# A slot-routing layer on eight cores: weight groups loaded in iterations 8 to 14, and the middle stage rearranged

## Time and profile before

| what | value |
|---|---|
| the profiled execution's own time | 314.32 us |
| its span, core 0 (the slowest) | 312.8 us |
| spans of the eight cores | 303.3 to 312.8 us |
| busy: PE, DVE, ACT, POOL | 72%, 64%, 57%, 53% |
| DMA queue q0 (issued by POOL) | 22.22 MB, 47.4% of 16 engines' span |
| DMA queue q1 (issued by SP) | 42.28 MB, 40.7% of 16 engines' span |
| loads of tiles 0 to 7 from DRAM (848) | 4 of 1024 KB |
| stores of the output (877) | 32 of 512 KB, 9.2 us to landing |

### The profile page before, as it was taken

The page is one execution under the profiler, slowest core; times in us unless marked ns, Lnnn a source line. Parts: engine busy times, 40 slices in busy tenths (PEclk is TensorE's granted clock), DMA queues, the critical chain, the costliest instruction groups (busy, mean ns, idle before and its releaser), DMA issues.

```text
span 312.8 us, 5721 instructions; the slowest of 8 cores (303.3 to 312.8 us)
## 1 busy us (share of the span) xinstructions
PE 223.8 (72%) x1784; PEld 131.7 (42%) x1806; DVE 201.7 (64%) x358; ACT 178.5 (57%) x332; POOL 164.6 (53%) x236
## 2 busy tenths in 40 slices
PE   0114769877998973696996999999478964888700
PEld 0001347653774751475774768864143420111000
DVE  1476787998895982479996566434522316999930
ACT  0117556793795883369797799541211028999800
POOL 3774897757775960888886758212000004656510
PEclk9999589998997998599997999999959996555555
DMA  7999999999999999999997000839999594999996
GB/s 184 269 233 184 233 214 238 229 245 259 253 301 206 216 234 268 189 244 168 160 174 117 1 3 8 130 51 147 179 161 176 168 337 190 353 345 353 351 353 246
DMA packets 23792, 65.43 MB, mean 209 GB/s; under 512 B 1958, under 2 KB 2470, under 8 KB 23762
## 3 DMA queue, kind: packets, MB, share of 16 engines
q0 software_dynamic: 11376, 22.22, 47.4%
q1 hardware_dynamic: 11584, 42.28, 40.7%
q10 hardware_dynamic: 802, 0.57, 0.6%
HBM read 66.30 MB, written 20.97 MB: 279 GB/s over the span
## 4 chain that ended last, share of the span: by engine, by line
DVE 31%; PE 30%; issue 11%; POOL 7%; DMA 7%; ACT 5%; another core or an unknown queue 3%; DVEq 1%; SPq 0%; POOLq 0%; ACTq 0%
DVE sb_x L875 10%; PE R L370 8%; PE R L546 4%; DMA sb_x<-x 4%; DVE sb_x L335 3%; DMA spk<-slotP 3%; DVE bn L284 3%; DVE bn L285 3%; POOL x1b L301 3%; PE R L354 2%; PE R L454 2%; PE R L315 2%; PE R L310 2%; DVE db L443 2%
## 5 line engine op out<-in xcount | busy, mean ns | idle before, releaser
L370 PE MATMUL R<-xT,w1a_s 128*128 128x256 bf16 x512 | 67.8, 281 | 1.7 <-DVE xT L362 1.7
L370 PEld LDWEIGHTS R<-xT,w1a_s 128*128 128x128 bf16 x512 | 50.4, 101 | 11.8 <-issue 2.2
L324 ACT ACTIVATE junk<-R 128x1024 bf16<-128x1024 f32 x32 | 32.6, 1020 | 38.3 <-PE R L320 38.1
L335 DVE SCALAR_TENSOR_TENSOR sb_x<-R,sqs,sb_x 128x1024 f32<-128x1024 f32 x32 | 40.9, 1278 | 18.0 <-POOL sqs L332 17.9
L347 POOL TENSOR_SCALAR x3b_s<-sb_x,nm,vr 128x1024 bf16<-128x1024 f32 x32 | 39.3, 1228 | 12.5 <-POOL vr L346 3.9
L875 DVE SCALAR_TENSOR_TENSOR sb_x<-R,sqs,sb_x 128x1024 f32<-128x1024 f32 x32 | 39.0, 1283 | 3.4 <-POOL sqs L873 3.4
L301 POOL TENSOR_SCALAR x1b<-sb_x,nm,r 128x1024 bf16<-128x1024 f32 x32 | 39.1, 1225 | 2.6 <-POOL r L295 1.8
L859 PE MATMUL R<-svd,aT 64*128 64x512 bf16 x64 | 29.3, 576 | 11.5 <-DVE sb_x L875 8.9
L339 ACT ACTIVATE junk<-sb_x,nm 128x1024 bf16<-128x1024 f32 x32 | 36.5, 1139 | 1.7 <-DVE sb_x L335 1.7
L867 ACT ACTIVATE x1b<-R 128x1024 bf16<-128x1024 f32 x32 | 32.8, 1024 | 5.3 <-PE R L859 2.4
L318 PE MATMUL R<-x1b,cmat 128*128 128x512 bf16 x32 | 14.0, 436 | 30.4 <-POOL x1b L301 30.4
(11 more groups left out here) (154 smaller groups left out, 355.7 us busy)
## 6 DMA issues: line engine op xcount, KB each, us to landing
sb_x<-x SPq DMA_DIRECT2D x19, 1024.0 KB, 24.4
out<-sb_x SPq DMA_DIRECT2D x32, 512.0 KB, 9.2
wsl<-wmid POOLq DMA_DIRECT2D x5, 1024.0 KB, 28.4
sb_x<-whh POOLq DMA_DIRECT2D x4, 1024.0 KB, 52.4
x<-sb_x SPq DMA_DIRECT2D x4, 1024.0 KB, 43.7
sb_x<-wmid POOLq DMA_DIRECT2D x4, 1024.0 KB, 34.8
msl<-wmid POOLq DMA_DIRECT2D x3, 1024.0 KB, 19.5
wsl<-whh POOLq DMA_DIRECT2D x2, 1024.0 KB, 66.7
```

Source lines behind the costliest of these rows:

```text
L324: kq[j] = AC.put(lambda a: a.activation(junk[:], RR[j % 2][:], AF.Square, scale=1.0 / 32.0, accum_out=sq[:, j:j + 1]), kC[j], tt.get("junk"))
L335: kx2[j] = DV.put(lambda v: v.scalar_tensor_tensor(xs(j), RR[j % 2][:], s2[:, j:j + 1], xs(j), op0=OP.mult, op1=OP.add), ks2[j], kx1[j])
L370: PE.quiet(lambda e, jc=jc, dc=dc, ob=ob, q=q: e.matmul(ob, w1a[:, dc * H + jc * P:dc * H + (jc + 1) * P], xT[:, (8 * (i % 2) + dc) * 2 * ...
```

## The change

**Front.** `LOAD_AT` is rewritten: group 2 moves from iteration 6 to 8, groups 3, 4, 5, 6 from 7, 8, 9, 12 to 11, 12, 13, 14; groups 0 and 1 stay at 10. The last four sums of alpha stand directly behind `weigh` in iteration 19, ahead of the last four `slot_in`, where before they stood at the head of iteration 20. **Slot rows.** `spk` becomes a view of the fifth buffer of `x1b`; its load and that of `bqk` are issued in iteration 16, and `spk` waits only for the last running sum. **Middle.** The gate n (722) goes ahead of the two operations on z, which are swapped and write 1 - z into `pr`; `alpha_t(0)` and `alpha_t(1)` go behind the tanh of n; v's projection stands directly behind the scores and ahead of the softmax; `alpha_t(3)` goes ahead of the copy of v; most `busy` groups are shorter (4, 6, 3, 6, 3, 10 become 2, 2, 3, none, 2, and 4 ahead of the moments' sum) and write to `BB`, so that they no longer wait for the copies of alpha. **wo by halves of the columns.** First all eight products of the left half, then those of the right; ACT copies each half with its own sum, and the mean is taken off by DVE (left) and ACT (right).

```diff
--- before.py
+++ after.py
@@ -174,6 +174,7 @@
         itau = sbt("itau", [P, 1])
         dnr = mv
         bn6 = sbt("bn6", [P, 24])
+        bqk = sbt("bqk_s", [P, 4])
         wsl = sbt("wsl", [P, NW * GC * D], BF16)
         x1b = sbt("x1b", [P, NX1 * D], BF16)
         tri, upr, one, eye = (cmat[:, k * P:(k + 1) * P] for k in range(4))
@@ -527,7 +528,7 @@
                      exps=exps, weigh=weigh)
         WHH_AT = {0: 1, 2: 2}
         SPILL_AT = {4: 0, 5: 1, 6: 2, 7: 3}
-        LOAD_AT = {6: (2,), 7: (3,), 8: (4,), 9: (5,), 10: (0, 1), 12: (6,)}
+        LOAD_AT = {8: (2,), 10: (0, 1), 11: (3,), 12: (4,), 13: (5,), 14: (6,)}
         kspill = {}
         GATE_AT = {5: 0, 7: 1, 9: 2}
 
@@ -567,6 +568,10 @@
             if i in WHH_AT:
                 load_whh(WHH_AT[i])
 
+            if i == NP:
+                kbqk = SP.dma(sem("bqk"), lambda e: e.dma_start(out=bqk[:], in_=bqk_d))
+                kspk = SP.dma(sem("spk"), lambda e: e.dma_start(out=x1b[:, 4 * D:5 * D].bitcast(F32), in_=spk_d),
+                              kC[NT - 1])
             if i in SPILL_AT:
                 p = SPILL_AT[i]
                 kspill[p] = SP.dma(sem("x2"), lambda e, p=p: e.dma_start(
@@ -583,8 +588,6 @@
                 weight_sum(range(0, NT - 4))
             if i == NP + 3:
                 busy(16, SPARE, kx2[NT - 2])
-            if i == NP + 4:
-                kdn = weight_sum(range(NT - 4, NT))
             for name, off in ORDER:
 
                 if name == "stats" and 2 * i + 4 < NPAIRED:
@@ -599,6 +602,8 @@
                 n = 2 * i + off if name in BY_TILE else i + off
                 if 0 <= n < (NT if name in BY_TILE else NP):
                     STAGE[name](n)
+                if name == "weigh" and n == NP - 1:
+                    kdn = weight_sum(range(NT - 4, NT))
 
                 if name == "gelu_b" and i in GATE_AT:
                     g = GATE_AT[i]
@@ -615,7 +620,7 @@
         em = ExitStack()
         sbm = lambda name, shp, dt=F32: em.enter_context(nc.sbuf_tensor(name, shp, dt))
         msl = sbm("msl", [P, NMID * GC * D], BF16)
-        spk = sbm("spk", [P, H])
+        spk = x1b[:, 4 * D:5 * D].bitcast(F32)
         c_ps = sbm("cps", [P, P])
         aT = sbm("aT", [P, NP * P], BF16)
         siT = sbm("siT", [P, H], BF16)
@@ -627,7 +632,6 @@
         svf = wsl[:, 8 * D:10 * D].bitcast(F32)
         qd = sbm("qd", [P, 2 * P], BF16)
         kTs = sbm("kTs", [P, 2 * NS], BF16)
-        bqk = sbm("bqk_s", [P, 4])
         ebd = sbm("ebd", [P, P], BF16)
         ebT = sbm("ebT", [P, P], BF16)
         sm = sbm("smx", [P, 16])
@@ -651,9 +655,7 @@
         for g, free in ((8, (last_h,)), (9, (last_h, last_l, last_sqx)), (10, after_ab)):
             tw[g] = group("w", slot(g), wmid_d[g], *free)
 
-        kspk = SP.dma(sem("spk"), lambda e: e.dma_start(out=spk[:], in_=spk_d), *after_ab)
         kps = SP.dma(sem("ps"), lambda e: e.dma_start(out=c_ps[:], in_=cps_d), *after_ab)
-        kbqk = SP.dma(sem("bqk"), lambda e: e.dma_start(out=bqk[:], in_=bqk_d), *after_ab)
 
         busy(8, SPARE, kx2[NT - 2])
 
@@ -696,9 +698,6 @@
         t = DV.put(lambda v: v.tensor_tensor(pz, G_Z, pz, op=OP.add), kz, kgh[1])
         kzt = AC.put(lambda a: a.activation(pz, pz, AF.Tanh, scale=0.5), t)
 
-        kzs = DV.put(lambda v: v.scalar_tensor_tensor(spk[:], pz, 1.0, spk[:], op0=OP.add, op1=OP.mult), kzt, kspk)
-        komz = DV.put(lambda v: v.tensor_scalar(pz, pz, -0.5, 0.5, op0=OP.mult, op1=OP.add), kzs)
-
 
         kaT = {}
 
@@ -715,14 +714,17 @@
                             t, *after_ab)
 
         kn = proj(G_N, siT, 16, ksiT, "in", kx2[NT - 2])
-        alpha_t(0)
-        busy(4, SPARE, kaT[0])
-        alpha_t(1)
-        busy(6, SPARE, kaT[1])
         t = DV.put(lambda v: v.scalar_tensor_tensor(hn, hn, 0.5, G_N, op0=OP.mult, op1=OP.add), kn, khn)
         kgn = t
+
+        komz = DV.put(lambda v: v.tensor_scalar(pr, pz, -0.5, 0.5, op0=OP.mult, op1=OP.add), kzt)
+        kzs = DV.put(lambda v: v.scalar_tensor_tensor(spk[:], pz, 1.0, spk[:], op0=OP.add, op1=OP.mult), kzt, kspk)
         t = AC.put(lambda a: a.activation(hn, hn, AF.Tanh), t)
-        t = DV.put(lambda v: v.tensor_tensor(hn, hn, pz, op=OP.mult), t, komz)
+        alpha_t(0)
+        busy(2, BB, kzt)
+        alpha_t(1)
+        busy(2, BB, kzt)
+        t = DV.put(lambda v: v.tensor_tensor(hn, hn, pr, op=OP.mult), t, komz)
         ksn = DV.put(lambda v: v.scalar_tensor_tensor(snb, spk[:], 0.5, hn, op0=OP.mult, op1=OP.add), t, kzs, *after_ab)
         ksnf = DV.put(lambda v: v.scalar_tensor_tensor(hn, spk[:], 0.5, hn, op0=OP.mult, op1=OP.add), ksn)
 
@@ -760,7 +762,7 @@
                     PE.quiet(fn, tw[c // GC], *ksnT, kgn)
         kqk = kuse[27]
         alpha_t(2)
-        busy(3, SPARE, kaT[2])
+        busy(3, BB, kzt)
         for kc2 in range(2):
             tq = DV.put(lambda v, k=kc2: v.tensor_scalar(
                 qd[:, k * P:(k + 1) * P].rearrange("p (u s) -> p u s", s=NS),
@@ -777,8 +779,9 @@
                 PE.quiet(fn, tq, tk, kx2[NT - 1])
             else:
                 t = PE.put(fn)
-        busy(6, SPARE)
-        t = DV.put(lambda v: v.tensor_reduce(sm[:, 0:1], SC, axis=AX, op=OP.max), t)
+        ksc = t
+        kvp = proj(BA, snT, 28, ksnT[0], "bv", kr, khn)
+        t = DV.put(lambda v: v.tensor_reduce(sm[:, 0:1], SC, axis=AX, op=OP.max), ksc)
         t = DV.put(lambda v: v.tensor_scalar(sm[:, 1:2], sm[:, 0:1], -1.0, None, op0=OP.mult), t)
         for h in range(2):
             te = AC.put(lambda a, h=h: a.activation(
@@ -789,12 +792,10 @@
         kebT = DV.put(lambda v: v.tensor_copy(ebT[:], XB[:, 0:P]), t)
         tt["xb"] = [kebT]
 
-        kvp = proj(BA, snT, 28, ksnT[0], "bv", kr, khn)
-        busy(3, SPARE)
+        alpha_t(3)
+        busy(2, BB, kzt)
         kvb = AC.put(lambda a: a.activation(vb[:], BA, AF.Identity), kvp, kn)
         kav = PE.put(lambda e: e.matmul(BB, ebT[:], vb[:], start=True, stop=True), kebT, kvb, kzt)
-        alpha_t(3)
-        busy(10, SPARE, kaT[3])
         GB, BB2 = SI, R1[:, 0:H]
         kgg = add_rows(GB, "g", True, ksiT)
         kgg = add_rows(BB2, "b", True, ksiT)
@@ -806,6 +807,7 @@
         t = DV.put(lambda v: v.bn_aggr(st3[:, 0:2], bn6[:, 0:6]), t)
         t = DV.put(lambda v: v.tensor_tensor(st3[:, 2:3], st3[:, 0:1], st3[:, 0:1], op=OP.mult), t)
         PSM = R1[:, H:H + 3]
+        busy(4, SPARE, kaT[3])
         t = PE.put(lambda e: e.matmul(PSM, c_ps[:], st3[:, 0:3], start=True, stop=True), t, kps)
         busy(14, SPARE)
         t = DV.put(lambda v: v.tensor_copy(sm[:, 4:7], PSM), t)
@@ -828,18 +830,23 @@
         S2 = R0
         for h in range(2):
             add_rows(S2[:, h * H:(h + 1) * H], f"bo{h}", True, tk, kaT[3])
-        for dc in range(8):
-            for h in range(2):
+
+        ks2v = {}
+        for h in range(2):
+            for dc in range(8):
                 fn = lambda e, dc=dc, h=h: e.matmul(
                     S2[:, h * H:(h + 1) * H], svT[:, dc * P:(dc + 1) * P], wch(44 + dc)[:, h * H:(h + 1) * H],
                     start=False, stop=(dc == 7), skip_group_check=True)
-                if dc == 7 and h == 1:
-                    ks2v = PE.put(fn)
+                if dc == 7:
+                    ks2v[h] = PE.put(fn)
                 else:
                     PE.quiet(fn, tw[(44 + dc) // GC], *ksvT)
-        t = AC.put(lambda a: a.activation(svf, S2[:], AF.Identity, accum_out=sm[:, 11:12]), ks2v, *after_ab)
-        t = DV.put(lambda v: v.tensor_scalar(sm[:, 12:13], sm[:, 11:12], -1.0 / D, None, op0=OP.mult), t)
-        ksvd = DV.put(lambda v: v.tensor_scalar(svd[:], svf, sm[:, 12:13], None, op0=OP.add), t)
+            t = AC.put(lambda a, h=h: a.activation(svf[:, h * H:(h + 1) * H], S2[:, h * H:(h + 1) * H], AF.Identity,
+                                                   accum_out=sm[:, 11 + h:12 + h]), ks2v[h], *after_ab)
+        kmean = DV.put(lambda v: v.tensor_scalar(sm[:, 13:14], sm[:, 11:12], sm[:, 12:13], -1.0 / D,
+                                                 op0=OP.add, op1=OP.mult), t)
+        ksvd = [DV.put(lambda v: v.tensor_scalar(svd[:, 0:H], svf[:, 0:H], sm[:, 13:14], None, op0=OP.add), kmean),
+                AC.put(lambda a: a.activation(svd[:, H:D], svf[:, H:D], AF.Identity, bias=sm[:, 13:14]), kmean)]
 
 
 
@@ -860,13 +867,13 @@
                     R[:, h * H:(h + 1) * H], aT[r:r + NS, (j // 2) * P:(j // 2 + 1) * P],
                     svd[r:r + NS, h * H:(h + 1) * H], start=True, stop=True)
                 if h == 0:
-                    PE.quiet(fn, ksvd, kaT[j // 8], kf.get(turns[u - 4]) if u >= 4 else None)
+                    PE.quiet(fn, *ksvd, kaT[j // 8], kf.get(turns[u - 4]) if u >= 4 else None)
                 else:
                     kP[j] = PE.put(fn)
             junk2 = svT
             t = AC.put(lambda a, R=R, j=j: a.activation(junk2, R[:], AF.Square, scale=1.0 / 32.0,
```

(2 more changed lines are left out.)

## The result

The changed kernel took 304.61 us (median of four runs, 302.84 to 305.02) beside 312.36 us for the kernel before on the same chip (four runs, 311.76 to 313.81): ratio 0.973, 95% interval 0.968 to 0.979. It is faster by 7.8 us. I had forecast 15.6 less, 296.9 us with a range from 292.5 to 304; the time lies just above that range. The profiled execution took 302.84 us and had a span of 301.2 us.

What follows compares the result with a forecast made beforehand. It took POOL's waits for spills to hold the front, the slot rows' load the middle and DMA stores the end; 10.5 (front) and 5.1 (middle and end) off the 312.48 us median gave 296.9 us, range 292.5 to 304.

Steps and rivals of the forecast that it cites:

- `spk` away from group 12: Weights before the end: without the 256 KB slot-row load beside it, group 12 lands 1.0 us earlier.
- idle time filled: Before the end: earlier stores fill the 4.1 us in which DMA idled between the loads of tiles 0 to 7 and the stores.
- Front: 10.5 us less: Iterations 7 and 9: moving groups 3 to 6 removes POOL's waits for spills; 10.5 us less, bounds 6 and 13.
- What is late next: Front, after the holes: x of tile 28, landing still at 137.6, has 10.6 us of slack, so DVE waits 0.2.
- Iteration 7's wait of 4.57 us: Front: PE's order hides POOL's wait for a spill, so removing it gains 0.1 us, bounds 0 and 4.6.
- the slower rival: Front: tile 28 lands late behind POOL's five groups and stops DVE, up to 15.8 us later; chance 0.03.
- The middle's terms: Middle: early alpha sums, slot rows, scores, softmax and v, moments and wo by halves save 8.8 us, bounds 4.8 and 10.
- this rival's condition: Middle: with fewer fillers the clock stays at half from the scores to the end of wo; 306 us, chance 0.07.
- The end bound by DMA: End, 264 to 309 us: DMA share 1.03 at 355 GB/s while DVE has room, so the stores bind.
- the loss of about 4: End: of the 8.8 us saved in the middle, 3.7 are lost because stores wait behind the tiles' loads.
- One sign of being wrong: End: the forecast would be wrong if DMA idles between group 12 and the stores.
- Something else takes over in the front: Front: tile 28 lands 4 to 5 us later, or ACT or POOL hold the pace; front 6, 301.4 us, chance 0.22.

Runs made afterwards that it cites:

- e6: The changed kernel with weight groups 3 and 4 loaded in iteration 12 and 5 and 6 in iteration 14, none in odd iterations: 301.97 us, ratio 0.965.
- e9: Changed kernel with even-iteration loads, tiles 0 and 1 back behind group 11, last whh product in iteration 11, not 9, weight loads at 10, 12, 14: 301.21 us, ratio 0.963.
- e7: The changed kernel without the 37 filler matmuls behind gate n's product: 305.0 and 305.1 us in two runs.
- e4: The changed kernel without the load of weight group 12, the second half of wo's chunks read from group 11: 301.86 us, ratio 0.955.
- e11: The changed kernel with the slot rows loaded a second time at the old place, into a tensor nobody reads: 303.99 us, ratio 0.971.
- e1: The kernel before with only the new LOAD_AT: 309.01 us, ratio 0.978.
- e2: The changed kernel with the old LOAD_AT, so the middle alone: 313.55 us, ratio 0.992.
- e5: The changed kernel measured a second time, nothing altered: 303.25 us, ratio 0.970.

## Why the prediction was right in sign and half in size

I take the sum of the forecast as it stands: 15.6 = 10.5 (front) + 1.0 (`spk` away from group 12) + 4.1 (idle time filled). On the core from which it was read, core 0, it came to 6.9 (group 8 issued at 205.42, then 198.50) + 0.5 (group 8's issue to the return, 38.55 to 38.07) + 4.3 (the return to the end, 68.8 to 64.5) = 11.7. In the mean over the cores the same three terms came to 5.6 (204.2, then 198.6), -0.2 (36.9 to 37.1) and 3.2 (66.7 to 63.5), together 8.7, and the time gained 7.8. So half of the missing 7.8 us was lost on core 0 itself, and the other half lies in having summed on that core of that execution.

**The step that failed: "Front: 10.5 us less".** Its two parts failed apart.

*What is late next.* The hole was priced nearly rightly on core 0: make_x2 of tile 19 stands 10.3 sooner (forecast 10.8, iteration 7's 0.1 among it), though L444 in iteration 9 now takes 1.24 us and not 0.42, which the forecast didn't have. I then asked only whether x would be late, and looked at no engine in iterations 10 to 13, though the change puts POOL's issues just there. These gave 3.4 back: 0.7 in iteration 10, where DVE waits for a scale behind two issues (the [0.92 <-POOL sqs L333] above), which the change left in their place and for which DVE had no wait before; 0.67 and 0.66 in iterations 11 and 13, where L444 grows from 1.24 to 1.91 and 1.89; and 1.6 at tiles 23 and 24, behind iteration 11, where alpha is later for PE than before; 0.2 came back. Windows of the changed kernel's core 0 and PE's row there:

```profile
136.00:138.00 2.00, 0.00 (x0) 0.00 (x0) 1.90 (x2) 1.91 (x6) 1.95 (x3) 1.00 1.05 162
138.00:140.00 2.00, 0.48 (x10) 0.38 (x11) 1.69 (x6) 1.16 (x3) 0.98 (x2) 0.99 1.07 157
140.00:142.00 2.00, 2.00 (x6) 0.72 (x5) 1.90 (x4) 0.00 (x0) 1.71 (x2) 0.50 1.01 138
142.00:144.00 2.00, 2.00 (x25) 1.71 (x24) 1.70 (x5) 1.49 (x4) 0.65 (x1) 0.66 1.12 164
```
```profile
139.52 0.39 PE L455 MATMUL R<-alpha,x3b_s 128*128 128x64 bf16 x8 [3.93 <-DVE alpha L447]
```

PE stands 3.93 us and then runs at half the clock until about 143. Before, it stood 2.57 us at this place, and the clock stayed full (PE's row, and the window around it):

```profile
148.47 0.39 PE L454 MATMUL R<-alpha,x3b_s 128*128 128x64 bf16 x8 [2.57 <-DVE alpha L446]
```
```profile
148.00:150.00 2.00, 1.53 (x15) 0.86 (x16) 1.90 (x5) 1.48 (x4) 1.25 (x2) 1.00 1.08 177
```

e6 shows the part of POOL's issues in this: with the loads out of the odd iterations 1.8 us of the mean's 2.5 come back. What the half clock costs can be read from e6 too, since two of its cores kept the full clock behind the same idle time and six lost it. PE and a window of core 0, which kept it, then of core 1:

```profile
138.85 0.39 PE L455 MATMUL R<-alpha,x3b_s 128*128 128x64 bf16 x8 [3.25 <-DVE alpha L447]
140.00:142.00 2.00, 2.00 (x29) 1.63 (x28) 2.00 (x4) 1.27 (x3) 1.70 (x3) 1.00 0.99 150
```
```profile
140.94 0.39 PE L455 MATMUL R<-alpha,x3b_s 128*128 128x64 bf16 x8 [3.24 <-DVE alpha L447]
142.00:144.00 2.00, 2.00 (x21) 1.34 (x20) 1.91 (x4) 0.85 (x1) 1.22 (x2) 0.52 0.97 174
```

From tile 19 to tile 23 these cores took 20.2 and 21.3 us: the half clock costs 1.1. In the kernel before, the clock fell at this place on five cores, behind 1.91 to 2.77 us, and stayed on three, core 0 among them, behind 1.80 to 2.57 (20.8 against 19.5 us); in the changed kernel it fell on all eight. So the length of PE's idle time alone doesn't decide it, and core 0 gave back more than the mean, 3.4 against 2.5, in part because it was one of the three.

*One core.* The hole between make_x2 of tiles 17 and 19 lasted 22.0 us on core 0, but 17.7 to 21.2 on the others, 19.6 in the mean; now all cores take 11.8 to 12.1. The cores gained 7.5 there in the mean (with 0.6 ahead of it 8.2), and 5.6 were left at group 8. The middle took 45.7 us on core 0 and 40.9 on four others, and now takes 35.9 to 36.9 on all. The change took away what made core 0 the slowest in that execution, and what core 0 gained beyond the mean gained nothing. It isn't a trait of core 0: in the eleven executions of the kernel before beside e9 the slowest was core 2 four times, core 0 three times, core 6 twice, and cores 3 and 4 once each. I had written "other cores had shorter holes but were up to 9.5 us shorter; I expect them just below": they weren't below. With the mean in place of core 0's number the front's term would have been 8.2 instead of 10.5, and the forecast 299.2. The 2.5 given back and the 2.1 by which the two other terms fall short of 5.1 in the mean bring it to 303.8, beside 304.6 measured.

**Right, by its steps.** Iteration 7's wait of 4.57 us cost next to nothing: make_x2 of tile 17 stands 0.5 sooner on core 0 (forecast 0.1). Tile 28 didn't wait, and landed after 36.8 us against 39.6: the slower rival is refuted. The middle's terms held on core 0 (8.9 against 8.3 behind `si`, and 0.5 ahead of it), the clock stayed full to the end of `wo`, and e7 shows that this rival's condition was real: without fillers it goes to half. Its price is borne out roughly: it had the middle 4 us longer than before, 3.3 of them in fillers that e7 doesn't have, and e7 has 43.2 against 42.8. The end bound by DMA is shown by e4, and the loss of about 4 by the changed kernel itself. `spk`'s 1.0 was 0.7 to 1.1 by e11, but between the kernels only 0.5 of it arrived on core 0 and nothing in the mean; why is open. One sign of being wrong that the forecast named did appear, DMA idle between group 12 and the stores; it had been there before, so it isn't what changed.

**The rivals.** "Something else takes over in the front" (301.4, front 6) is the nearest, and its 6 is near what core 0 (6.9) and the mean (5.6) gained; of its causes POOL holding the pace is the one that e6 bears out. Its time was still 3 us too low, since it too was summed on core 0.

What the end makes of a gain can be put in one rule for the runs in which the tiles come back together, fitted to their means: the span is the later of first product + 54 and return + 63.5. Before: 307.7 and 304.6, measured 307.8. Changed: 295.2 and 299.2, measured 299.1. e7: 302.0 and 298.6, measured 302.1. e1: 304.3 and 302.7, measured 304.6. e2: 302.9 and 307.0, measured 306.8. e4: 296.5 and 293.4, measured 296.2. e5: 294.0 and 297.6, measured 297.8. e11: 295.8 and 299.9, measured 299.5. e6: 294.0 and 296.8, measured 295.9, the largest miss. The two constants are read from these same runs, so only the agreement among them is a test. So before the change the first product was the bound, by 3 us, and now DMA is, by 4: this is the crossing at which the middle's gain stops counting.

## What to carry to other kernels

Where several cores run the same program and the time is that of the slowest, read a wait on every core before pricing its removal, and sum with the mean: the core that the profile shows is the slowest of one execution, with the largest waits of it, and it stops being the slowest once they are gone. Where a load's issue is moved, look at what stands around its new place on the issuing engine, and at which instruction of another engine shares a data path with that. And where an end has two starts, of the transfers and of the compute, keep one line for each: a gain counts only up to the other.

## What the runs showed of the hardware beyond what I expected

A VectorE multiply of 128x256 float32 with both inputs in SBUF took 0.43 us alone, 1.23 beside one of POOL's 1.20 us operations, and 1.91 with a DMA issue of 0.79 us ahead of that operation. At one point of the loop the granted clock fell to 0.50 on five of eight cores behind PE idle times of 1.91 to 2.77 us, on six of eight behind 3.25 us (e6) and on all eight behind 3.9 us; the cores that kept 1.00 had 1.80 to 2.57 and 3.25 us, and were 1.1 us (e6) to 1.3 us (before) faster over four tiles. And 37 matmuls of 512 columns whose result nobody reads kept the first product of the end 6.8 us sooner.
